# Expert rows of a mixture-of-experts block: loaded in four feature parts and turned by VectorE

## What is computed

```
logits = x @ w_router;  top 2 of 8;  scores = softmax(top 2)
for e in range(8):
    h1 = rows_of_expert_e @ fc1_w[e]            # 256 -> 512
    proj, gate = split(h1)                      # 256 and 256
    out_rows = silu(proj) * gate @ fc2_w[e]     # 256 -> 256
moe_out[token] = sum over its 2 rows of score * out_row
out = x + tanh(g_ffn) * (moe_out + shared_mlp)
```

## Time and profile before

| what | value |
|---|---|
| median of 3 runs | 330.27 us (327.27 to 334.4) |
| the profiled execution | 327.38 us |
| its span | 325.6 us |
| granted TensorE clock, mean | 0.993 |
| busy PE, DVE, ACT, POOL | 303.2, 242.1, 168.8, 130.4 us |
| PE's share of the span | 93% |
| expert tiles, from the first to the last transposition of rows | 182.7 to 280.6 us |

### The profile page before, as it was taken

One profiled execution on the slowest core, in us unless ns is written; L12 is line 12 of the kernel. 1 busy time (PEld: TensorE's weight loads), 2 busy tenths in 40 slices (PEclk: granted clock), 3 DMA queues, 4 the chain that ended last, 5 costly groups with the idle time before them and its releaser, 6 DMA issues.

```text
span 325.6 us, 8082 instructions
## 1 busy us (share of the span) xinstructions
PE 303.2 (93%) x2505; PEld 244.4 (75%) x2505; DVE 242.1 (74%) x728; ACT 168.8 (52%) x322; POOL 130.4 (40%) x151
## 2 busy tenths in 40 slices
PE   8948889999989979999999799999999999999986
PEld 8727677787868765655585578888889988888865
DVE  5576597698999998688799966666566666534895
ACT  2543767767778655357694145444444444424131
POOL 5732144232374655415771187633433333421000
PEclk9998999999999999999999999999999999999999
DMA  7892776676756553058256013323333233104941
GB/s 241 247 221 78 235 200 193 170 244 166 234 162 190 155 160 105 34 178 294 87 175 144 8 46 100 107 91 98 91 105 101 90 94 96 65 16 156 414 141 64
DMA packets 34069, 47.18 MB, mean 145 GB/s; under 512 B 5519, under 2 KB 27667, under 8 KB 33522
## 3 DMA queue, kind: packets, MB, share of 16 engines
q1 hardware_dynamic: 28706, 34.61, 35.5%
q0 software_dynamic: 4320, 10.92, 10.1%
q10 hardware_dynamic: 1008, 1.18, 1.2%
HBM read 22.20 MB, written 12.62 MB: 107 GB/s over the span
## 4 chain that ended last, share of the span: by engine, by line
PE 41%; DVE 21%; issue 17%; POOL 9%; DMA 6%; SPq 3%; ACT 2%; POOLq 0%; DVEq 0%; ACTq 0%
PE ps L1748 26%; POOL dispatched L541 4%; DVE x_all L1335 3%; DVE fc_lo L1178 3%; DMA stacks<-work 3%; PE ps L1794 2%; SPq L381 2%; PE ps L1720 2%; PE ps L1598 2%; DMA expert_rows<-v_s,slot_u 2%; PE ps L1578 2%; DMA stacks<-expert_rows 2%; POOL rs L526 2%; DVE fc_lo L1184 1%; PE ps L1408 1%
## 5 line engine op out<-in xcount | busy, mean ns | idle before, releaser
L597 POOL DMA_INDIRECT expert_rows<-v_s,slot_u x39 | 38.3, 981 | 59.2 <-ACT v_s L868 43.7
L964 DVE TENSOR_REDUCE mx<-ps 128x8 f32<-128x1024 f32 x32 | 39.1, 1223 | 13.2 <-PE ps L1438 12.6
L549 POOL TENSOR_TENSOR work<-work 128x512 bf16<-128x512 f32 x16 | 18.5, 1155 | 49.7 <-ACT work L646 49.7
L1285 DVE TENSOR_TENSOR act<-ps,sil 128x256 f32<-128x256 f32 x39 | 16.5, 424 | 28.8 <-ACT sil L861 28.6
L677 ACT ACTIVATE probs<-ps 128x1024 f32<-128x1024 f32 x32 | 32.7, 1021 | 9.2 <-PE ps L1471 9.2
L861 ACT ACTIVATE sil<-ps 128x256 f32<-128x256 f32 x39 | 15.0, 384 | 41.4 <-PE ps L1748 41.3
L1748 PE MATMUL ps<-fc_hi,xs_hi 128*128 x78 | 34.2, 439 | 1.4 <-DVE xs_lo L1266 1.4
L1748 PE MATMUL ps<-fc_hi,xs_lo 128*128 x78 | 30.7, 394 | 0.0
L1748 PE MATMUL ps<-fc_lo,xs_hi 128*128 x78 | 30.7, 394 | 0.0
L868 ACT ACTIVATE v_s<-ps,wt 128x256 f32<-128x256 f32 x39 | 18.5, 474 | 19.6 <-PE ps L1748 19.6
L1438 PE MATMUL ps<-stacks 96*128 96x128 bf16 x256 | 20.1, 222 | 7.1 <-DMA stacks<-work 3.5
(11 more groups left out here) (221 smaller groups left out, 820.3 us busy)
## 6 DMA issues: line engine op xcount, KB each, us to landing
stacks<-work SPq DMA_DIRECT2D x75, 128.0 KB, 2.7
xs_in<-dispatched SPq DMA_DIRECT2D x39, 129.0 KB, 2.0
fc_s<-in_fc SPq DMA_DIRECT2D x8, 512.0 KB, 5.0
stacks<-work POOLq DMA_DIRECT2D x18, 128.0 KB, 3.4
ctx_s<-in_ctx_t SPq DMA_DIRECT2D x8, 256.0 KB, 3.5
fc_s<-in_fc SPq DMA_DIRECT2D x8, 256.0 KB, 5.1
stacks<-expert_rows SPq DMA_DIRECT2D x2, 1024.0 KB, 6.0
probs<-expert_rows SPq DMA_DIRECT2D x2, 1024.0 KB, 10.1
```

What stands on the lines that cost most here:

```text
L549: nc.gpsimd.tensor_tensor(out[:, 2, :], rest, out[:, 1, :], ALU.subtract).then_inc(ready, 1)
L597: nc.gpsimd.indirect_dma_start(ys, bass.IndirectOffsetOnAxis(dst_u[:, r:r + 1], 0), y_out[:, r, :], None, bounds_check=2 * T - 1, oob_is_e ...
L964: nc.vector.reduce_max(mx[:, j, 8 * h:8 * h + 8], ps_s, AX_X).then_inc(max_ok[j][h], 1)
L1285: nc.vector.tensor_tensor(act[:, par], ps[:, 2 + par, FI:2 * FI], sil[:, par], ALU.mult).then_inc(act_ok, 1)
```

## The change

From tile 4 on (`BY_PE` = 4) PE no longer transposes the rows. Three DMAs of SP and one of ACT load a tile in four feature parts: part q, the features 64q to 64q+63 of 128 tokens, goes to the 32 partitions 32q to 32q+31, four tokens to a partition. Then one DVE instruction transposes all 32x32 blocks of the tile, which leaves features on the partitions and tokens along the row (`xs_t`, in SBUF). The features come out in another order than before, so the host orders the rows of `fc1` accordingly. ACT and DVE read `xs_t` in place of PSUM. For the first four tiles, which PE still transposes, the features are loaded in that order by two DMAs.

The two extra words are loaded by a DMA of their own into `ends_in`, eight buffers deep. They hold the integer place and the score as they are used, so the two small DVE operations of each tile are gone, and their waits too. SP waits, from tile 8 on, for the scatter of tile n-8 and the transposition of tile n-4. ACT now also reads the row numbers into registers, in each stretch of `expert_steps`. `HEAD` is 8: eight tiles written out, three turns of the loop, seven tiles.

```diff
-HEAD = 5
+HEAD = 8
+BY_PE = 4
...
+        def rows_t(t, d):
+            par = (t.c + d) % 2
+            if isinstance(t.i, int) and t.c + d < BY_PE:
+                return ps[:, par, 0:2 * P].rearrange("p (k t) -> p k t", k=2)
+            return xs_t[:, par]
...
+        def quarter(t, q, row):
+            tokens = xs[bass.ds(row, P), D // 4 * q:D // 4 * (q + 1)].rearrange("(i p) f -> p i f", p=32)
+            return xs_in[32 * q:32 * q + 32, t % 4, :].rearrange("p (i f) -> p i f", i=4), tokens
...
             def load_tile(t, row):
                 r = t.c % 4
-                if t.since(4):
+                if t.since(4 + BY_PE):
+                    scattered, turned = held(sp, t.laps(0, -1)), held(sp, t.n(-3 - BY_PE))
+                    sp.wait_ge(ysc[r], scattered)
+                    sp.wait_ge(turned_ok, turned)
+                elif t.c >= 4:
                     sp.wait_ge(xst_done, t.n(-3))
-                    sp.wait_ge(dst_ok, t.n(-3))
-                sp.dma_start(xs_in[:, r, :], xs[bass.ds(row, P), :]).then_inc(tile_in[r], 16)
+                if isinstance(t.i, int) and t.c < BY_PE:
+                    for k in range(2):
+                        sp.dma_start(xs_in[:, r, P * k:P * k + P].rearrange("p (q f) -> p q f", f=32),
+                                     xs[bass.ds(row, P), 0:D].rearrange("p (q k f) -> p q k f", k=2, f=32)[:, :, k]
+                                     ).then_inc(tile_in[r], 16)
+                else:
+                    for q in range(3):
+                        to, of = quarter(t.c, q, row)
+                        sp.dma_start(to, of).then_inc(tile_in[r], 16)
+                sp.dma_start(ends_in[:, t.c % 8, :], xs[bass.ds(row, P), D:D + 2]).then_inc(tile_in[r], 16)
...
-            def step(t):
+            def last_quarter(n, row):
+                at, of = quarter(n.c, 3, row)
+                if n.since(4 + BY_PE):
+                    sa.wait_ge(turned_ok, n.n(-3 - BY_PE))
+                else:
+                    sa.wait_ge(xst_done, n.n(-3))
+                sa.dma_start(at, of).then_inc(tile_in[n.c % 4], 16)
+
+            def rows_ahead(i, c, n):
+                c, n = c + 6, min(n, NT - c - 6)
...
+                loaded = nc.values_load_multi_w_load_instructions(
+                    at, engines=[mybir.EngineType.Activation], min_val=0, max_val=NULL_ROW,
+                    skip_runtime_bounds_check_because=CLAMPED)[1]
...
+                if t.c + 6 < NT:
+                    last_quarter(Tile(t.i, t.c + 6), row)
...
+            def expert_turn(t, d):
+                n = Tile(t.i, t.c + d)
+                ve.wait_ge(tile_in[n.c % 4], arrived(n))
+                if n.since(2 + BY_PE):
+                    ve.wait_ge(xst_ok, n.n(-1))
+                    ve.wait_ge(xlo_ok, n.n(-1))
+                nc.vector.transpose(xs_t[:, n.c % 2].rearrange("p k (i t) -> p k i t", t=32),
+                                    xs_in[:, n.c % 4, :].rearrange("p (i k f) -> p k i f", k=2, f=32)
+                                    ).then_inc(turned_ok, 1)
...
                     expert_act(t, 1)
-                    expert_dst(t, 1)
                 expert_actt(t)
+                if BY_PE <= t.c + 3 < NT:
+                    expert_turn(t, 3)
...
-                if n + 2 < NT:
+                if n + 2 < BY_PE:
                     expert_x(t, 2)
```

More of the change, by code:

```diff
@@ L220, in build_program @@
         hid_1 = v_s[:, :, :, :].rearrange("p a j e -> p (a j) e")
-        xs_in = nc.alloc_sbuf_tensor_at("xs_in", [P, 4, ROW], F32, offset=start["row_s"])
+        xs_in = nc.alloc_sbuf_tensor_at("xs_in", [P, 4, D], F32, offset=start["row_s"])
+        xs_t = nc.alloc_sbuf_tensor_at("xs_t", [P, 2, 2, P], F32, offset=start["wq_s"])
         o0 = 4 * ROW
@@ L331, in live, with arrived @@
             return 0 <= g < G
+        def rows_t(t, d):
[3 more added lines that the diff above has]
+            return xs_t[:, par]
+        def arrived(t, d=0):
+            n = t.c + d
+            if isinstance(t.i, int):
+                return sum(48 if m < BY_PE else 80 for m in range(n % 4, n + 1, 4))
+            return t.i * 160 + 48 + 80 * (n // 4)
+        def quarter(t, q, row):
+            tokens = xs[bass.ds(row, P), D // 4 * q:D // 4 * (q + 1)].rearrange("(i p) f -> p i f", p=32)
+            return xs_in[32 * q:32 * q + 32, t % 4, :].rearrange("p (i f) -> p i f", i=4), tokens
         def expert_steps(eng, body, load=None):
@@ L338, in run @@
                 for r in range(n):
-                    body(Tile(i, c + r), *([values[r]] if load else []))
+                    body(Tile(i, c + r), *([values[r] if r < len(values) else None] if load else []))
             turns = (NT - HEAD) // TURN
@@ L445, in _ @@
                 load_second(e)
-            sp.wait_ge(zero_row_ok, 1)
+            sp.wait_ge(zero_row_ok, 3)
             sp.wait_ge(pads_ok, 1)
@@ L848, in rows_in_halves @@
                 par = (t.c + d) % 2
-                sa.wait_ge(xst_done, t.n(d + 1))
+                if isinstance(t.i, int) and t.c + d < BY_PE:
+                    sa.wait_ge(xst_done, t.n(d + 1))
+                else:
+                    sa.wait_ge(turned_ok, t.n(d + 1 - BY_PE))
                 if t.since(2 - d):
                     sa.wait_ge(h_done, t.n(d - 1))
-                nc.scalar.activation(xs_hi[:, par],
-                                     ps[:, par, 0:2 * P].rearrange("p (k t) -> p k t", k=2),
-                                     ACT.Copy).then_inc(xst_ok, 1)
+                nc.scalar.activation(xs_hi[:, par], rows_t(t, d), ACT.Copy).then_inc(xst_ok, 1)
             def expert_silu(t, d):
@@ L880, in step @@
                     high_half(xt_hi[:, 2 * c - 4:2 * c - 2, :], xt_all[:, :, CH * P * c:CH * P * (c + 1)])
+                if t.c + 6 < NT:
+                    last_quarter(Tile(t.i, t.c + 6), row)
+            early = nc.values_load_multi_w_load_instructions(
+                base_i[0:1, 4:6], engines=[mybir.EngineType.Activation], min_val=0, max_val=NULL_ROW,
+                skip_runtime_bounds_check_because=CLAMPED)[1]
             rows_in_halves(Tile(0, 0), 0)
             rows_in_halves(Tile(0, 0), 1)
+            for n in (4, 5):
+                last_quarter(Tile(0, n), early[n - 4])
             expert_silu(Tile(0, 0), 0)
-            expert_steps(sa, step)
+            expert_steps(sa, step, rows_ahead)
             gate_silu(2, 0, 1)
@@ L1265, in expert_rows @@
                     ve.wait_ge(h_done, t.n(d - 1))
[L1266 to L1278, removed]
+                nc.vector.tensor_tensor(xs_lo[:, par], rows_t(t, d), xs_hi[:, par].bitcast(F32),
+                                        ALU.subtract).then_inc(xlo_ok, 1)
+            def expert_turn(t, d):
[7 more added lines that the diff above has]
+                                    ).then_inc(turned_ok, 1)
             def expert_act(t, d):
@@ L1862 @@
     w_q, w_kv = np.asarray(L0_xattn_Wq), np.asarray(L0_xattn_Wkv)
-    fc1, fc2 = tiles(L0_ffn_fc1_w, 128), tiles(L0_ffn_fc2_w, 128)
+    fc1, fc2 = np.asarray(L0_ffn_fc1_w), tiles(L0_ffn_fc2_w, 128)
+    fc1 = fc1.reshape(-1, 4, 2, 32, fc1.shape[-1]).transpose(1, 3, 0, 2, 4)
     arrays = {
```

37 lines of the change are left out of this document (21 added, 16 removed).

## The result

The changed kernel takes 341.08 us (median of 6 runs, 339.66 to 343.58), the kernel before 331.5 (6 runs beside it, 327.27 to 334.4). The ratio is 1.0355, with a 95% interval of 1.0312 to 1.0397: slower by 3 to 4%. It is taken over the runs of the faster of two states that executions show and is not the quotient of the two medians, which alone give 1.029; the sign is the same by either. The forecast was 326.5. The profiled execution took 340.31 us with a span of 338.5, which is 12.9 more than the span before.

What follows compares the result with a forecast made beforehand. The prediction took SP's DMA issue to bound the kernel from the middle of the tiles on: 327.4 profiled, less 1.5 by SP, plus 0.6 for a near tie, gave 326.5 us, with a range of 322 to 348.

Steps and rivals of the forecast that it cites:

- computing as 3.5 us of gain: Expert tiles without SP's limit: -6.8 ring, -0.1 small DVE operations, +3.4 ACT register loads, -3.5 us in all.
- dear part loads: Rival on SP: a part load costs 0.61 like ctx, SP needs 3.28 us a tile, 346 us; chance 0.33.
- a slow transposition: Rival on DVE: the 32x32 transposition runs at half rate, ring 2.64 us, total 333 us; chance 0.1.
- PE, 0.23 us a tile: TensorE in the expert tiles: two transposes fewer save 0.23 us, so PE alone could go at 2.31 a tile.
- The transposition, 0.42: DVE's 32x32 block transposition of a tile: taken as a 256-column operation out of SBUF, 0.42 us.
- The ring of DVE and ACT, 2.37: Transposition, xs_hi, xs_lo, act, act_hi, act_lo and back to the next transposition: 2.37 us a tile.
- The ring becomes the bound of the computing: Over 34 expert tiles, 2.37 us a tile on DVE and ACT against 2.57 before: 6.8 us gained.
- ACT's register load, 1.0 a turn: ACT's load of eight row numbers makes xs_hi 1.0 us late at each of three loop turns, 3.0 in all.
- ACT's DMA issue, nothing: ACT's one DMA a tile: its 0.41 us issue lies beside the scaling and costs nothing, uncovered 0.2 at most.
- So SP decides: SP's DMA issue, 2.68 us a tile with 0.41 per part load, sets the end: -1.5 us where computing allows -3.5.
- SP doesn't matter: Rival: part loads at 0.39 or less, or a longer lead, let computing decide: 324 us; chance 0.15.
- DMA engines, hidden: The DMA engines' load of smaller packets: 1.7 us of 2.6 a tile with the scatter's share, hidden.

Runs made afterwards that it cites:

- the reordered kernel: Changed kernel with DVE's transposition of tile n+3 moved ahead of act_hi and act_lo of tile n: 335.44 us, ratio 1.0161 to the kernel before.
- the PSUM experiment: Changed kernel with the transposition written into the PSUM bank TensorE's transposes used, not SBUF: 333.53 us, ratio 1.0092 to the kernel before.
- The last two repaired kernels: Changed kernel with transposition into PSUM and ahead of the conversions: 330.12 us; the same with ACT loading one row number per tile: 325.88 us.
- the kernels with five DMAs on SP: SP issues all four parts, ACT no DMAs or row numbers: on the changed kernel 344.41 us, with transposition into PSUM and ahead of the conversions 341.21 us.
- The repairs measured one by one: Each alone on the changed kernel: transposition into PSUM 333.53 us, transposition ahead of the conversions 335.44 us, ACT loading one row number per tile 337.22 us.
- the repaired kernel with five DMAs a tile: Changed kernel with transposition into PSUM and ahead of the conversions, SP issuing all four parts, ACT no DMAs or row numbers: 341.21 us, ratio 1.0343.
- the kernel with the pieces: Changed kernel with GpSimd's two 128x1024 subtractions cut into eight of 128x256: 335.59 us, ratio 1.0167 to the kernel before.

## Why the prediction was wrong

It took SP as what decides and computing as 3.5 us of gain. Both were wrong, the second more. That 341 lies within the stated 322 to 348 is luck: the upper part of that range stood for dear part loads and a slow transposition, and neither came.

- **PE, 0.23 us a tile: right within 0.03.** In the reordered kernel every other tile takes 2.34, so the two transposes cost 0.20 to 0.21. In the tiles between, the second products begin 0.07 to 0.09 late, and the mean pace is 2.38 to 2.39 and not 2.31.
- **The transposition, 0.42: right within 0.02** (0.434). Its rival at half rate is out. The Trainium skill's figure ("VectorE: DVE Perf Modes", "The three transpose paths") led to an estimate of 0.44, which was closer.
- **The ring of DVE and ACT, 2.37: right as far as it goes** (2.38 in the rows above), **but the step "The ring becomes the bound of the computing" failed.** It left out the loop through TensorE, 2.555, that the new order of DVE closes. This took the gain of 6.8 away but for 0.4. The reordering alone gives the pace back, and no other edit does.
- **The largest error is not a term of the sum but a missing one.** I priced `xs_lo` out of SBUF as 0.45 and asked nothing about who else reads SBUF then. It cost 7.5 us by the PSUM experiment: two stalls of 2.56 and 2.60, and by the granted clock the rest in the steps behind them at the lower level. The row for it stood in the trace of before, GpSimd's `xt_lo` of 2.42 us beside `xs_lo`. The Trainium skill has the rule ("SBUF — State Buffer", "Who interferes with whom"): a DVE instruction with two SBUF inputs contends with a GpSimd instruction that reads SBUF, one of them waits for the whole of the other, and one with a single SBUF input does not, outside its modes with two ports. The traces agree for the long operation (3.0 us with both inputs in SBUF, 0.42 with one in PSUM). Beside pieces a quarter as long they agree in one place of six (1.01 us, to 0.29 behind GpSimd's end); in the other five, at 0.66 to 0.78, DVE's row ended before GpSimd's.
- **ACT's register load, 1.0 a turn: the mechanism was right, the size was not.** It measures 1.24, 1.55 and 1.55. From the start of the scaling to the `xs_hi` behind it are 242.21 - 239.32 = 2.89 us at the turn and 247.42 - 246.01 = 1.41 elsewhere, 1.48 more. I had the load end 2.5 behind the scaling's start: the load is 1.76 and not 1.68, the branch puts it at 0.95 and not 0.8, and 0.18 of register work follows it. The load among the first tiles was priced at 0.4. The last two repaired kernels, which differ in ACT's register loads alone, take 7.08 and 6.48 from tile 0 to tile 3: 0.6.
- **ACT's DMA issue, nothing: right.** 0.32 a tile behind the start of the scaling; with it TensorE still reaches 2.39.
- **SP: failed.** "So SP decides" rested on 0.41 for a part load. It is 0.317, with 0.50 from one to the next. A tile takes 2.17, and by the estimate above 2.45 with turns and long issues, in place of 2.68. SP then waits for others: 18.3 us for scatters. The condition that the prediction named for the rival "SP doesn't matter", a part load of 0.39 or less, was met. That rival's mechanism held and its time of 324 did not, since its computing was the same wrong sum. Of the rule that went with it ("DMA: Bandwidth & Descriptors", "Issuing engines are not separate DMA queues"), that issuing is usually small, the change shows one side and the kernels with five DMAs on SP the other: there it costs 0.5 us a tile and is the bound.
- **DMA engines, hidden: right.** Their share from 230 to 290 us is 0.43, about 1.1 us a tile; I had 1.7.

As a sum: -6.8 for the ring became -0.4, +3.0 for the turns became +4.3, SP's part went, and +8.2 came in between tiles 0 and 9; with the first tile 0.9 later that is 13.0, and the spans differ by 12.9. The repairs measured one by one (7.5, 5.6, 3.9) sum to 17 and give 324; together they gave 325.9.

## What to carry to other kernels

When an operand moves from PSUM to SBUF, look at what GpSimd does at that time before pricing the operation: the cheapest repair here was to let VectorE write its transposition into the PSUM bank that TensorE had left. When a stage moves to another engine, follow each loop round to where it closes, across tiles and through the engine that was relieved, and choose its place in that engine's order by the longest of them. A load of many registers stands in the queue of the engine that needs it as one block; one at a time it hid.

## What else the runs showed of the hardware

- SP's load of eight row numbers took 1.67 to 1.84 us before. In the change its three loads of eight in the loop took 0.53 or 0.54 each and the one of seven behind the loop 1.19, while ACT's of eight took 1.76. No run says why.
- In all changed kernels but the reordered one (which had one), four to seven DMA issues of SP took 0.6 to 2.1 us in place of 0.32 to 0.37, those over 1 us 16 to 20 us apart in the repaired kernel with five DMAs a tile. In the kernel before, none of 39 did. What causes them stays open.
- DVE was released about 0.29 us after GpSimd's 128x1024 subtraction ended by the profile, in all eight collisions of the four kernels that have them. In seven of them DVE's row had started 0.21 to 0.55 us before GpSimd's, and it was DVE that was held all the same.
- After 2.35 us without products TensorE's products came at the lower clock (0.43 apart) for 3.6 us, so a stall of DVE can cost more than its length. In the kernel with the pieces, where no `xs_lo` was longer than 1.01 us, the clock stayed at 1.00 from 200 to 230 us.
